# Diagonals of B written by DMA and loaded back, and a ring of states longer by a triple

## The chip, the cores and the metric

The kernel runs on one core of a Trainium2 chip. The metric is the device time of one execution in microseconds (us), lower is better; several runs are given by their median. The engines are PE (TensorE; PEld is its weight load), DVE (VectorE), ACT (ScalarE), POOL (GpSimd) and SP (SyncE), whose queue issues the DMAs.

## The reference

The input is x of 4 x 32 x 32 x 384, in f32. Two residual blocks follow each other.

```python
x = x + ssm_block(group_norm(x))        # conv + four-direction selective scan
x = x + moe_block(group_norm(x))        # router, top 2 of 4 experts, GELU
```

In the first block the projected input passes a 3 x 3 depthwise convolution and SiLU and becomes u. For each of 4 images and 4 directions (rows or columns, forward or backward) a selective scan over the 1024 positions is computed for 192 channels, with 16 states each:

```python
dA  = exp(dt[..., None] * A)                       # 192 channels x 16 states
h   = h * dA + (dt * u)[..., None] * B[:, None, :] # B: 16 values for a position
y   = einsum('bkcn,bkn->bkc', h, C)
```

B and C are projections of u and differ from position to position. Then follow a norm, a gate and a projection back. The second block's expert weights w1 and w2 are 384 x 384 each.

## The kernel before

There are three parts: `head` (norm, projection, convolution, projections of B, C and dt), `scan` and `tail` (norm and gate, output projection, experts).

`scan` handles 16 units, one for each image b, orientation o and direction s (unit u = 4b + 2o + s). A unit has 24 steps. Its 16 states are taken as 8 pairs n, and a pair with the 192 channels gives a triple of 3 steps (groups g of 64 channels, one state of the pair on each half of the partitions). All engines run their own instruction order and meet at semaphores:

- PE, `spread_b(u, i)`: (dt * u) times B, for the step's 128 partitions and 1024 positions, into the PSUM tile `pb` (two slots). B is applied by matmuls whose right side is a diagonal: for each state n and each of 8 blocks of positions (BLK = 8) the tile `dd` holds, on partition p of two halves of 64, row p of diag(B) (64 x 64 floats). `dd` is 128 partitions x 8192 floats and lies in `area`. A step is 32 such products (64 matmul records).
- DVE, `step_h(step)`: the scan itself, from `a` (the decay exp(dt A), made by ACT in `decay`) and `pb` into `h`. `h` has room for TRIPLES = 3 triples. Scan of triple n waits until triple n - TRIPLES has been added up (`y_added`).
- POOL, `times_c`: h times C, two instructions a triple; the rows of C come to `crow` by DMA (`load_crow`, 3 slots).
- PE, `add_y`: sums the triple into `py` and `py2` through an identity, LAG = 7 steps behind spread_b. It stands after spread_b of its step in PE's order.
- At the change of orientation `take_y` moves the sums out: at step 6, on DVE in units 2, 6, 10 and 14 (followed by `carry` on PE), on ACT in units 4, 8 and 12.

Beside a unit the next one is prepared, a chunk a step, PE into the PSUM tile `pm` and ACT out of it: Z (dt) at steps 0 to 3, BT (B with the positions on partitions, into `bt`) at step 4, UT (u; only before an even unit) at 5 to 8, DUP at 16 to 19. ACT does abs, exp and 1 + e at steps 4 to 6 and logarithms at 9, 11, 13; DVE does softplus at steps 9 to 14 and `times_u` (L294) after step 15.

The diagonals come from `bt` times `mask`, a constant with ones where j equals the partition (modulo 64). `dd` has four pieces of four states. POOL builds pieces 1 and 3 (`build_d`, L199, one instruction a piece), ACT pieces 0 and 2 (`build_rows`, L284, 32 instructions a piece, two or three a step). A piece is rebuilt when spread_b has used it up (6 steps a piece, `b_row`). For unit 0 pieces 0 and 1 are built in the head by POOL.

SP issues all DMAs in one written order. In the scan, for each n: crow, then at n = 0 the rows of dt and B of the next unit (`load_rows`) and sometimes u (`load_u`), at n = 3 sometimes `store_y`, at n = 7 `double`, a copy between halves of `dup`. crow of pair n waits until POOL is done with pair n - 3. Constants (KEPT) are loaded in the head, w1 and w2 among them.

Of the kernel before, what the change touches and what calls it, by code (L numbers as in the profile page):

```python
# [11 lines left out]
P = 128  # L12
BATCH = 4
# [18 lines left out]
PR = 32  # L32
KEPT = ("wout", "gam", "bet", "wr", "rb", "w1", "b1", "w2", "b2", "spread", "eyeb", "wdt", "apar", "dpar", "mask", "ones")
PROJ = 4
# [6 lines left out]
CROWS = 3  # L41
TRIPLES = 3
LAG = 7
# [4 lines left out]
Y_STORED = 16 * 3  # L48
LAST_U = UNITS - 1
KINDS = (2, 0, 1)  # L50
XD = ((0, 2, 1, 3), (0, 1, 2, 3))
# [63 lines left out]
def load_rows(sp, d, keep, shared, u):  # L115

    b, o, s = unit_of(u)
    rows = keep["rows"]
    sp.dma_start(rows[0:R], d["xd"][b, o, s * PR:s * PR + R]).then_inc(shared["rows_in"], 16)
    sp.dma_start(rows[PR:PR + N], d["xd"][b, o, 2 * PR + s * N:2 * PR + (s + 1) * N]).then_inc(shared["rows_in"], 16)  # L120

# [25 lines left out]
class Units:  # L147

    def __init__(self, nc, ctx, keep, ys, shared):
# [15 lines left out]
        self.dtut = sb("dtut", [P, 2, BLK, DI])  # L165
        self.bt = sb("bt", [P, 2, N, BLK])
        self.amin = sb("amin", [P, UNITS // BATCH * STEPS])
# [21 lines left out]
        self.d_odd = sem("d_odd")  # L189
        self.b_row = sem("b_row")  # L190
        self.dup_in = [sem(f"dup_in{g}") for g in range(CG)]

    def build_d(self, eng, tt, u, piece):

        eng.wait_ge(self.chunk_taken, CHUNK[u, "BT", 0] + 1)
        need(eng, self.b_row, STEPS * (u - 1) + 6 * (piece + 1) if u else 0)
        rows_n = slice(4 * piece, 4 * piece + 4)
        shape = [P, 4 * BLK, HALF]
        tt(self.dd[:, rows_n].rearrange("p n k j -> p (n k) j"),  # L199
           self.bt[:, u % 2, rows_n].rearrange("p n k -> p (n k)").unsqueeze(2).broadcast_to(shape),  # L200
           self.keep["mask"][:].unsqueeze(1).broadcast_to(shape), ALU.mult).then_inc(self.d_odd if piece % 2 else self.d_even, 1)
# [9 lines left out]
    def chunk(self, pe, u, what, i):  # L211
# [4 lines left out]
        if what == "Z":  # L216
            pe.wait_ge(self.shared["rows_in"], 16 * 2 * (u + 1))
# [23 lines left out]
    def take_chunk(self, act, u, what, i):  # L241

        nc, pm = self.nc, self.pm
        act.wait_ge(self.chunk_done, CHUNK[u, what, i] + 1)
        if what == "Z":
            need(act, self.dtu_ready, u)
            need(act, self.dt_ready, ROUNDS * u)
            dst, src = self.zs[:, 2 * DI * i:2 * DI * (i + 1)], pm[:, 0:2 * DI]
        if what == "BT":
            need(act, self.d_even, 2 * (u - 1))  # L250
            need(act, self.d_odd, 2 * (u - 1))
            dst = self.bt[:, u % 2].rearrange("p n k -> p k n")
# [23 lines left out]

    def build_rows(self, act, u, piece, lo, hi):

        if lo == 0:
            act.wait_ge(self.chunk_taken, CHUNK[u, "BT", 0] + 1)  # L280
            need(act, self.b_row, STEPS * (u - 1) + 6 * (piece + 1) if u else 0)
        for at in range(lo, min(hi, 4 * BLK)):
            n, blk = 4 * piece + at // BLK, at % BLK
            row = self.nc.scalar.activation(self.dd[:, n, blk], self.keep["mask"][:], ACT.Identity,  # L284
                                            scale=self.bt[:, u % 2, n, blk:blk + 1])
        if hi >= 4 * BLK:
            row.then_inc(self.d_even, 1)
# [111 lines left out]
def head(nc, d, keep, keep_from, ys, m, shared):  # L399
# [5 lines left out]
    with ExitStack() as ctx:  # L405
# [271 lines left out]
        def _(act):  # L677
# [111 lines left out]
            act.wait_ge(turned, NC * BATCH)  # L789
            m.build_rows(act, 0, 2, 0, 2 * BLK)  # L790

# [91 lines left out]
        def _(pool):  # L883
# [3 lines left out]
            for piece in range(2):  # L887
                m.build_d(pool, nc.gpsimd.tensor_tensor, 0, piece)


def scan(nc, d, keep, ys, m, norm, shared):

    with ExitStack() as ctx:
# [42 lines left out]
        def _(sp):  # L936
# [18 lines left out]
            for u in range(UNITS):  # L955
                b, o, s = unit_of(u)
                for n in range(NP):
                    load_crow(u * NP + n)
                    if n == 0 and u + 1 < UNITS:
                        sp.wait_ge(chunk_done, CHUNK[u, "BT", 0] + 1)  # L960
                        load_rows(sp, d, keep, shared, u + 1)
# [25 lines left out]
        def _(pe):  # L987
            def spread_b(u, i):
# [5 lines left out]
                if i % 6 == 0:  # L994
                    piece = i // 6
                    pe.wait_ge(d_odd if piece % 2 else d_even, 2 * u + piece // 2 + 1)
                need(pe, h_ready, step - 1)
# [67 lines left out]
        def _(act):  # L1065
# [29 lines left out]
            for u in range(UNITS):  # L1095
                b, o, s = unit_of(u)
                for i in range(STEPS):
# [3 lines left out]
                    if u + 1 < UNITS:  # L1101
# [85 lines left out]
        def _(pool):  # L1187
# [8 lines left out]
            for u in range(UNITS):  # L1196
                for n in range(NP):
                    times_c(u * NP + n, range(0, 2))
                    times_c(u * NP + n, range(2, CG))
                    if n == 1:  # L1200
                        m.build_d(pool, nc.gpsimd.tensor_tensor, u, 3)
                    if n == 4 and u + 1 < UNITS:
                        m.build_d(pool, nc.gpsimd.tensor_tensor, u + 1, 1)


def tail(nc, d, keep, ys, norm, shared):
# [8 lines left out]
    with ExitStack() as ctx:  # L1215
# [3 lines left out]
        def sem(name):  # L1219
            return ctx.enter_context(nc.semaphore("t_" + name))  # L1220

        eye, gavg, wout, gam, bet, wr, rb, w1, b1, w2, b2, spread, eyeb = (
            keep[k] for k in ("eye", "gavg", "wout", "gam", "bet", "wr", "rb", "w1", "b1", "w2", "b2", "spread", "eyeb"))
        yg = sb("yg", [P, KIND, L])
# [30 lines left out]

        xt_in = [sem(f"xt_in{b}") for b in range(BATCH)]
        small_taken = sem("small_taken")
        back_done = sem("back_done")
# [89 lines left out]
        def _(sp):  # L1348
# [23 lines left out]
        def _(pe):  # L1372
# [71 lines left out]

            def first_layer(b, j):
                for q in halves():
                    for c in range(NC):
# [17 lines left out]
            def second_layer(b, t):  # L1465
                if t == 0:
                    pe.wait_ge(hw_ready, NC * (b + 1))
                    pe.wait_ge(b2_ready, 5)
# [242 lines left out]
def kept(nc, ctx, d):  # L1711

    def sb(name, shape, dt=F32):
# [5 lines left out]
        gam=sb("gam", [P, DI]), bet=sb("bet", [P, DI]), wr=sb("wr", [P, NC, EXPERTS]), rb=sb("rb", [P, EXPERTS]),  # L1719
        w1=sb("w1", [P, NC, C]), b1=sb("b1", [P, NC]), w2=sb("w2", [P, NC, C]), b2=sb("b2", [PIECES * PR, C]),  # L1720
        spread=sb("spread", [PR, C], BF16),
# [10 lines left out]
    from_dram = dict(wout=d["wout"], gam=d["ln_g"].partition_broadcast(P), bet=d["ln_b"].partition_broadcast(P), wr=d["wr"],  # L1732
                     rb=d["rb"].partition_broadcast(P), w1=d["w1"], b1=d["b1"], w2=d["w2"], b2=d["b2"], spread=d["spread"],
                     eyeb=d["eyeb"], wdt=d["wdt"], apar=d["apar"], dpar=d["dpar"], mask=d["mask"], ones=d["ones"])
# [3 lines left out]
def bass_vision_mamba_moe(nc, x, eye, win, wx, gavg, conv_p, ones, wdt, apar, dpar, mask, wout, ln_g, ln_b, wr, rb, w1, b1, w2, b2, spread, eyeb, out):  # L1738
    def scratch(name, shape, dt=F32):
# [7 lines left out]
        xt=scratch("xt", (BATCH, NC, P, L)), sz=scratch("sz", (PAIRS, P, TT, 2 * DI)),  # L1747
        xd=scratch("xd", (BATCH, 2, P, L)), u=scratch("u", (PAIRS, KIND, P, L)), ub=scratch("ub", (PAIRS, 2, KIND, P, L)), y=scratch("y", (PAIRS, KIND, P, L)),
    )
# [110 lines left out]
```

## Time and profile before

| | |
|---|---|
| median of 3 runs | 1642.54 us (1640.47 to 1648.41) |
| profiled execution, its own time | 1650.07 us |
| its span, first to last instruction | 1648.3 us |
| busy: PE, PEld | 1349.6 us (82%), 824.1 (50%) |
| busy: DVE, ACT, POOL | 1229.3 (75%), 1014.8 (62%), 1026.4 (62%) |
| mean granted PE clock | 0.942 of full speed |
| DMA | 73478 packets, 151.08 MB, mean 92 GB/s |

Busy shares are means over stages with different limits. PE's records are pipelined, so its busy share is no measure of how full it is.

### The profile page before, as it was taken

What the parts mean: (1) busy time and instruction counts of PE and PEld (TensorE: products, weight loads), DVE (VectorE), ACT (ScalarE), POOL (GpSimd) and SP (SyncE); (2) the same over time, 40 slices, a digit from 0 to 9 for tenths busy, and PEclk for the clock granted to TensorE, in tenths of its full rate; (3) what the DMA queues carried; (4) which work ended last, traced back from release to release, by engine and by line L of the source; (5) the groups of instructions that cost most, each with busy time, mean ns of one, the idle gap of its engine ahead of it and who ended that gap; (6) DMA issues with size and microseconds to landing.
All of it is one profiled execution on the core that took longest, in us unless ns stands there. A gap on an engine that the chain in (4) does not pass through costs nothing. (4 is left out here: it accounts for less than half of the span.)

```text
span 1648.3 us, 66375 instructions
## 1 busy us (share of the span) xinstructions
PE 1349.6 (82%) x30408; PEld 824.1 (50%) x30408; DVE 1229.3 (75%) x1025; ACT 1014.8 (62%) x1916; POOL 1026.4 (62%) x294
## 2 busy tenths in 40 slices
PE   6997779687886979788697878869787867879998
PEld 5734546444554545455454545545454534436554
DVE  4984298979798897989889798888979884733220
ACT  2558578766777877677787767777776640402222
POOL 0002189879797988889798889979888870000000
PEclk8998689999999999999999999999999997879999
DMA  9334324323232432323343232324323325101101
GB/s 324 125 148 185 112 65 107 96 67 96 54 90 73 110 91 72 96 68 90 74 109 86 77 91 73 90 73 109 86 77 81 97 81 196 39 0 39 39 29 48
DMA packets 73478, 151.08 MB, mean 92 GB/s; under 512 B 33238, under 2 KB 41942, under 8 KB 72816
## 3 DMA queue, kind: packets, MB, share of 16 engines
q1 hardware_dynamic: 73200, 146.83, 30.3%
q8 instruction: 240, 3.93, 1.0%
q14 instruction: 38, 0.31, 0.1%
HBM read 101.72 MB, written 32.51 MB: 81 GB/s over the span
## 5 line engine op out<-in xcount | busy, mean ns | idle before, releaser
L1193 POOL TENSOR_TENSOR s_h<-s_h,s_crow 128x2048 f32<-128x2048 f32 (+1 forms) x256 | 880.2, 3469 | 198.0 <-DVE s_h L1158 197.9
L1158 DVE TENSOR_TENSOR_SCAN s_h<-s_a,s_pb 128x1024 f32<-128x1024 f32 x384 | 864.2, 2277 | 183.6 <-PE s_py L1041 78.5
L1002 PE MATMUL s_pb<-k_area,m_dtut 64*64 64x64 f32 x24576 | 470.2, 224 | 194.2 <-DVE s_h L1158 162.8
L1002 PEld LDWEIGHTS s_pb<-k_area,m_dtut 64*64 64x64 f32 x24576 | 424.1, 138 | 384.6 <-DVE s_h L1158 230.1
L1041 PE MATMUL s_py<-s_h,k_eye 64*64 64x512 f32 x3072 | 417.8, 603 | 20.4 <-ACT y_y L1090 15.6
L284 ACT ACTIVATE k_area<-k_mask,m_bt 128x64 f32<-128x64 f32 x992 | 273.9, 337 | 0.0
L1084 ACT ACTIVATE s_a<-y_y,m_aneg 128x1024 f32<-128x1024 f32 x192 | 218.6, 1139 | 39.9 <-DVE s_h L1158 39.8
L1084 ACT ACTIVATE s_a<-m_dup,m_aneg 128x1024 f32<-128x1024 f32 x192 | 219.5, 1143 | 29.7 <-DVE s_h L1158 29.7
L199 POOL TENSOR_TENSOR k_area<-m_bt,k_mask 128x2048 f32<-128x2048 f32 x33 | 145.8, 4419 | 126.1 <-ACT m_bt L262 126.1
L1041 PEld LDWEIGHTS s_py<-s_h,k_eye 64*64 64x64 f32 x3072 | 90.1, 137 | 33.3 <-ACT y_y L1090 16.0
L262 ACT COPY y_y<-m_pm 128x384 f32<-128x384 f32 (+1 forms) x96 | 49.2, 513 | 91.8 <-PE m_pm L219 79.2
L1070 ACT ACTIVATE m_pm<-y_y 128x512 f32<-128x512 f32 x45 | 26.8, 596 | 98.5 <-DVE y_y L1141 98.5
L219 PEld LDWEIGHTS m_pm<-k_wdt,k_rows 25*128 25x128 f32 x256 | 42.4, 196 | 56.9 <-issue 56.5
L1473 PE MATMUL t_small<-k_w,k_area 128*128 128x384 f32 x192 | 70.4, 504 | 0.0
L1538 ACT COPY t_out<-t_small 128x384 f32<-128x384 f32 x32 | 15.3, 479 | 88.4 <-PE t_small L1476 88.4
L1448 PE MATMUL t_big<-t_xn,k_w 128*128 128x512 f32 x144 | 67.9, 623 | 0.0
L219 PE MATMUL m_pm<-k_wdt,k_rows 25*128 25x192 f32 x256 | 62.5, 366 | 6.5 <-DMA k_rows<-scratch_xd 6.5
L805 DVE SCALAR_TENSOR_TENSOR h_acc<-h_xpad,h_conv_p,h_acc 128x1024 f32<-128x1024 f32 x48 | 61.7, 1285 | 1.6
L238 PEld LDWEIGHTS m_pm<-k_eye,y_y 64*64 64x64 f32 (+1 forms) x512 | 33.6, 123 | 52.9 <-issue 49.9
L1659 DVE TENSOR_TENSOR k_area<-k_area,t_big 128x1024 f32<-128x1024 f32 x12 | 14.3, 1219 | 50.6 <-PE t_big L1462 50.4
L1473 PEld LDWEIGHTS t_small<-k_w,k_area 128*128 128x128 f32 x192 | 37.0, 197 | 18.5 <-issue 1.9
L238 PE MATMUL m_pm<-k_eye,y_y 64*64 64x64 f32 (+1 forms) x512 | 42.9, 224 | 2.7 <-ACT y_y L262 2.7
(189 smaller groups left out, 1233.5 us busy)
## 6 DMA issues: line engine op xcount, KB each, us to landing
s_crow<-scratch_xd SPq DMA_DIRECT2D x256, 256.0 KB, 4.0
k_area<-in_x_dram SPq DMA_DIRECT2D x4, 1536.0 KB, 8.0
scratch_xt<-y_y SPq DMA_DIRECT2D x4, 1536.0 KB, 10.2
y_y<-y_y SPq DMA_DIRECT2D x24, 256.0 KB, 3.6
m_dup<-m_dup SPq DMA_DIRECT2D x24, 256.0 KB, 3.2
out_dram<-t_out SPq DMA_DIRECT2D x32, 192.0 KB, 1.9
k_area<-scratch_xt SPq DMA_DIRECT2D x3, 1536.0 KB, 6.9
scratch_xd<-h_dbl SPq DMA_DIRECT2D x8, 512.0 KB, 2.6
```

Source lines behind the costliest of these rows:

```text
L199: tt(self.dd[:, rows_n].rearrange("p n k j -> p (n k) j"), self.bt[:, u % 2, rows_n].rearrange("p n k -> p (n k)").unsqueeze(2).broadcast_ ...
L219: mm = pe.matmul(pm[:, x * DI:(x + 1) * DI], tokens(rows[0:R + 1], 2 * i + x), self.keep["wdt"][:, o + 2 * s], start=True, stop=True)
L238: mm = pe.transpose(pm[0:chans.stop - chans.start, blk::BLK], self.dt_of[here, blk, chans], eye[here, here])
L284: row = self.nc.scalar.activation(self.dd[:, n, blk], self.keep["mask"][:], ACT.Identity, scale=self.bt[:, u % 2, n, blk:blk + 1])
L805: eng.scalar_tensor_tensor(out, view, w, out, ALU.mult, ALU.add).then_inc(convolved[kind], 1)
L1002: mm = pe.matmul(pb[par * HALF:(par + 1) * HALF, step % 2, r * BANK + blk:(r + 1) * BANK:BLK], dtut[here, u % 2, blk, g * HALF:(g + 1) * H ...
L1041: mm = pe.matmul(dst, eye[here, here], src, start=opens, stop=closes)
L1084: nc.scalar.activation(a[:, step % RING], dup[u % 2][:, g], ACT.Exp, scale=aneg[:, col:col + 1]).then_inc(a_ready, 1)
L1158: nc.vector.tensor_tensor_scan(h[:, step % (TRIPLES * CG), f], a[:, step % RING, f], pb[:, step % 2, f], 0.0, ALU.mult, ALU.add).then_inc( ...
L1193: nc.gpsimd.tensor_tensor(here, here, c.unsqueeze(1).broadcast_to([P, groups.stop - groups.start, L]), ALU.mult).then_inc(hc_ready, 1)
L1448: mm = pe.matmul(big_of("F1", b, j)[:, q], w1[:, c, j * P:(j + 1) * P], xn[:, b % 2, c, q], start=(c == 0), stop=(c == NC - 1))
L1473: pe.matmul(ps, hid[:, j, tok], w2[:, j], start=False, stop=False, skip_group_check=True)
```

## The change

- `dd` is built on the core for unit 0 only. Its four pieces are then stored to a new DRAM tensor `dd` (`store_d`), so that all off the diagonals is zero there. For each later unit `write_diagonal` copies the 4 x 8 x 64 x 2 values of B of a piece from `xd` in DRAM onto the diagonals in DRAM (two DMAs of 2048 elements of 4 bytes, each element 8196 bytes after the one before), and `load_d` loads the piece (1 MB) into `area` when the unit before has used it up. Piece 0, 1 and 2 are written at n = 2, 4, 6 and loaded at n = 3, 5, 7 of the unit before, piece 3 at n = 0 and 1 of its own unit.
- `build_d` and `build_rows` remain for unit 0; the BT chunk and B's rows are no longer made for units 1 to 15, and `bt` has one slot.
- TRIPLES is 4, not 3.
- w1 and w2 are loaded in the tail, behind the loads of xt; PE waits for them before the first and the second expert layer.

```diff
-TRIPLES = 3
+TRIPLES = 4
+QUARTER = 4 * BLK * HALF
...
-    order = [("Z", ch) for ch in range(4)] + [("BT", 0)]
+    order = [("Z", ch) for ch in range(4)]
+    if u == 0:
+        order += [("BT", 0)]
...
+    def write_diagonal(self, sp, d, u, piece):
+        b, o, s = unit_of(u)
+        sp.wait_ge(self.d_stored[piece] if u == 1 else self.d_in[piece], 16 * max(u - 1, 1))
+        there = d["dd"][piece]
+        first = 2 * PR + s * N + 4 * piece
+        rows = d["xd"][b, o, first:first + 4].rearrange("n (k r j) -> r (n k) j", r=2, k=BLK)
+        for r in range(2):
+            diagonal = bass.AP(tensor=there.tensor, offset=there.offset + r * HALF * QUARTER, ap=[[HALF, 4 * BLK], [QUARTER + 1, HALF]])
+            sp.dma_start(diagonal, rows[r], allow_slow_non_contiguous=True).then_inc(self.d_written[piece], 16)
+
+    def load_d(self, sp, d, u, piece):
+        sp.wait_ge(self.d_written[piece], 32 * u)
+        sp.wait_ge(self.b_row, STEPS * (u - 1) + 6 * (piece + 1))
+        sp.dma_start(self.quarter(piece), d["dd"][piece]).then_inc(self.d_in[piece], 16)
+
+    def store_d(self, sp, d, piece):
+        sp.wait_ge(self.d_odd if piece % 2 else self.d_even, piece // 2 + 1)
+        sp.dma_start(d["dd"][piece], self.quarter(piece)).then_inc(self.d_stored[piece], 16)
...
+                    if u == 0 and n < 4:
+                        m.store_d(sp, d, n)
+                    if n in (2, 4, 6) and u + 1 < UNITS:
+                        m.write_diagonal(sp, d, u + 1, (n - 2) // 2)
+                    if n in (3, 5, 7) and u + 1 < UNITS:
+                        m.load_d(sp, d, u + 1, (n - 3) // 2)
+                    if n == 0 and u:
+                        m.write_diagonal(sp, d, u, 3)
+                    if n == 1 and u:
+                        m.load_d(sp, d, u, 3)
...
-                        if 6 <= i < 18:
-                            m.build_rows(act, u + 1, 0, share(i - 6), share(i - 5))
-                        if i >= 18:
-                            m.build_rows(act, u + 1, 2, share(i - 18), share(i - 17))
-                    if i < 6:
-                        m.build_rows(act, u, 2, share(i + 6), share(i + 7))
+                    if u == 0 and i < 6:
+                        m.build_rows(act, 2, share(i + 6), share(i + 7))
...
-                    if n == 1:
-                        m.build_d(pool, nc.gpsimd.tensor_tensor, u, 3)
-                    if n == 4 and u + 1 < UNITS:
-                        m.build_d(pool, nc.gpsimd.tensor_tensor, u + 1, 1)
+                    if u == 0 and n == 1:
+                        m.build_d(pool, nc.gpsimd.tensor_tensor, 3)
...
+            sp.dma_start(w1[:], d["w1"]).then_inc(w1_in, 16)
+            sp.dma_start(w2[:], d["w2"]).then_inc(w2_in, 16)
```

## Rows read from the trace of the kernel before

**Rows 1.** Line L1158, the scans: ns min/median/max, first and last start; idle before, us and times.

```profile
L1158 DVE TENSOR_TENSOR_SCAN s_h<-s_a,s_pb x384: 2255/2280/2289, 187.6 to 1342.8; 128x1024 f32<-128x1024 f32 x192
...
  PE s_py L1041: 78.5, 72
  PE s_pb L1002: 63.2, 43
```

**Rows 2.** Groups by line and shape: busy us, mean ns | idle before.

```profile
L1193 POOL TENSOR_TENSOR s_h<-s_h,s_crow 128x2048 f32<-128x2048 f32 x128 | 583.0, 4554 | 188.8 <-DVE s_h L1158 188.6
...
L1193 POOL TENSOR_TENSOR s_h<-s_h,s_crow 128x1024 f32<-128x1024 f32 x128 | 305.0, 2383 | 9.3 <-DVE s_h L1158 9.2
L284 ACT ACTIVATE k_area<-k_mask,m_bt 128x64 f32<-128x64 f32 x992 | 273.9, 337 | 0.0
...
L199 POOL TENSOR_TENSOR k_area<-m_bt,k_mask 128x2048 f32<-128x2048 f32 x33 | 145.8, 4419 | 126.1 <-ACT m_bt L262 126.1
```

**Rows 3.** Waits by engine, 229 to 1318 us: us in total, times, longest.

```profile
PE s_pb L1002 <- issue: 25.0, 30, 3.6
...
SPq L943 <- POOL s_h L1193: 725.6, 117, 11.7
```

**Rows 4.** Timeline of an odd unit, steps 4 to 9: start, us, instruction.

```profile
711.91 0.81 PE L1002 MATMUL s_pb<-k_area,m_dtut 64*64 64x64 f32 x39
...
714.46 1.16 PE L1002 MATMUL s_pb<-k_area,m_dtut 64*64 64x64 f32 x64
...
726.67 1.16 PE L1002 MATMUL s_pb<-k_area,m_dtut 64*64 64x64 f32 x64
...
727.65 1.04 PE L1041 MATMUL s_py<-s_h,k_eye 64*64 64x512 f32 x8
...
728.86 2.29 DVE L1158 TENSOR_TENSOR_SCAN s_h<-s_a,s_pb 128x1024 f32<-128x1024 f32 x1 [1.73 <-PE s_py L1041]
```

**Rows 5.** Timeline of unit 4, steps 5 to 8, with ACT's take_y and SP's y2 stores.

```profile
495.44 1.50 ACT L269 ACTIVATE y_y<-y_y 128x1536 f32<-128x1536 f32 x1
...
497.00 1.11 PE L1002 MATMUL s_pb<-k_area,m_dtut 64*64 64x64 f32 x64
...
497.93 1.04 PE L1041 MATMUL s_py<-s_h,k_eye 64*64 64x512 f32 x8
...
498.79 1.11 PE L1002 MATMUL s_pb<-k_area,m_dtut 64*64 64x64 f32 x64
...
503.56 0.99 ACT L1089 COPY y_y<-s_py 128x1024 f32<-128x1024 f32 x1
...
505.44 4.33 SPq L952 DMA_DIRECT2D scratch_y<-y_y  x2
...
508.72 2.29 DVE L1158 TENSOR_TENSOR_SCAN s_h<-s_a,s_pb 128x1024 f32<-128x1024 f32 x1 [5.12 <-PE s_pb L1002]
```

**Rows 6.** DMA issues of the span: count, size, median us to landing.

```profile
k_area<-scratch_xt SPq DMA_DIRECT2D x3, 1536.0 KB, 6.9
...
k_u<-scratch_ub SPq DMA_DIRECT2D x16, 128.0 KB, 5.1
...
scratch_y<-y_y SPq DMA_DIRECT2D x8, 128.0 KB, 6.1
```

**Rows 7.** Windows: length; busy PE, PEld, DVE, ACT, POOL; clock, DMA share, GB/s.

```profile
695.00:701.00 6.00, 3.66 (x127) 2.37 (x126) 5.55 (x3) 4.28 (x9) 6.00 (x3) 1.00 0.82 215
588.00:594.00 6.00, 4.04 (x144) 2.31 (x144) 5.93 (x7) 3.91 (x8) 5.81 (x2) 1.00 0.76 216
```

**Rows 8.** Timeline of PE at 695 to 702 us: what stood inside groups of spread_b.

```profile
695.55 0.50 PE L1002 MATMUL s_pb<-k_area,m_dtut 64*64 64x64 f32 x18 [0.91 <-issue]
...
701.10 0.74 PE L1002 MATMUL s_pb<-k_area,m_dtut 64*64 64x64 f32 x34 [1.89 <-issue]
```

**Rows 9.** Page, part 3, DMA queues: packets, MB, share of 16 engines.

```profile
q1 hardware_dynamic: 73200, 146.83, 30.3%
q8 instruction: 240, 3.93, 1.0%
```

More of the change, by code:

```diff
@@ L32 @@
 PR = 32
-KEPT = ("wout", "gam", "bet", "wr", "rb", "w1", "b1", "w2", "b2", "spread", "eyeb", "wdt", "apar", "dpar", "mask", "ones")
+KEPT = ("wout", "gam", "bet", "wr", "rb", "b1", "b2", "spread", "eyeb", "wdt", "apar", "dpar", "mask", "ones")
 PROJ = 4
@@ L119, in load_rows @@
     sp.dma_start(rows[0:R], d["xd"][b, o, s * PR:s * PR + R]).then_inc(shared["rows_in"], 16)
-    sp.dma_start(rows[PR:PR + N], d["xd"][b, o, 2 * PR + s * N:2 * PR + (s + 1) * N]).then_inc(shared["rows_in"], 16)
+    if u == 0:
+        sp.dma_start(rows[PR:PR + N], d["xd"][b, o, 2 * PR + s * N:2 * PR + (s + 1) * N]).then_inc(shared["rows_in"], 16)
 def load_u(sp, d, keep, shared, b, what):
@@ L165, in __init__ @@
         self.dtut = sb("dtut", [P, 2, BLK, DI])
-        self.bt = sb("bt", [P, 2, N, BLK])
+        self.bt = sb("bt", [P, N, BLK])
         self.amin = sb("amin", [P, UNITS // BATCH * STEPS])
@@ L190, in __init__, with build_d @@
         self.b_row = sem("b_row")
+        self.d_in = [sem(f"d_in{piece}") for piece in range(4)]
+        self.d_stored = [sem(f"d_stored{piece}") for piece in range(4)]
+        self.d_written = [sem(f"d_written{piece}") for piece in range(4)]
         self.dup_in = [sem(f"dup_in{g}") for g in range(CG)]
-    def build_d(self, eng, tt, u, piece):
-        eng.wait_ge(self.chunk_taken, CHUNK[u, "BT", 0] + 1)
-        need(eng, self.b_row, STEPS * (u - 1) + 6 * (piece + 1) if u else 0)
+    def build_d(self, eng, tt, piece):
+        eng.wait_ge(self.chunk_taken, CHUNK[0, "BT", 0] + 1)
         rows_n = slice(4 * piece, 4 * piece + 4)
@@ L216, in chunk @@
         if what == "Z":
-            pe.wait_ge(self.shared["rows_in"], 16 * 2 * (u + 1))
+            pe.wait_ge(self.shared["rows_in"], 16 * (u + 2))
             for x in range(2):
@@ L249, in take_chunk @@
         if what == "BT":
-            need(act, self.d_even, 2 * (u - 1))
-            need(act, self.d_odd, 2 * (u - 1))
-            dst = self.bt[:, u % 2].rearrange("p n k -> p k n")
+            dst = self.bt[:].rearrange("p n k -> p k n")
             src = pm[:, 0:BLK * N].rearrange("p (k n) -> p k n", k=BLK)
@@ L275, in exponent, with quarter, build_rows @@
             nc.scalar.activation(self.wz, ez, ACT.Identity, bias=1.0).then_inc(self.w_ready, 1)
-    def build_rows(self, act, u, piece, lo, hi):
+    def write_diagonal(self, sp, d, u, piece):
[14 more added lines that the diff above has]
+        sp.dma_start(d["dd"][piece], self.quarter(piece)).then_inc(self.d_stored[piece], 16)
+    def quarter(self, piece):
+        return self.keep["area"][:].rearrange("p a l -> p (a l)")[:, piece * QUARTER:(piece + 1) * QUARTER]
+    def build_rows(self, act, piece, lo, hi):
         if lo == 0:
-            act.wait_ge(self.chunk_taken, CHUNK[u, "BT", 0] + 1)
-            need(act, self.b_row, STEPS * (u - 1) + 6 * (piece + 1) if u else 0)
+            act.wait_ge(self.chunk_taken, CHUNK[0, "BT", 0] + 1)
         for at in range(lo, min(hi, 4 * BLK)):
@@ L284, in build_rows @@
             row = self.nc.scalar.activation(self.dd[:, n, blk], self.keep["mask"][:], ACT.Identity,
-                                            scale=self.bt[:, u % 2, n, blk:blk + 1])
+                                            scale=self.bt[:, n, blk:blk + 1])
         if hi >= 4 * BLK:
@@ L789, in _ @@
             act.wait_ge(turned, NC * BATCH)
-            m.build_rows(act, 0, 2, 0, 2 * BLK)
+            m.build_rows(act, 2, 0, 2 * BLK)
         def convolve(eng, pair, kind, taps=range(9)):
@@ L887, in _ @@
             for piece in range(2):
-                m.build_d(pool, nc.gpsimd.tensor_tensor, 0, piece)
+                m.build_d(pool, nc.gpsimd.tensor_tensor, piece)
 def scan(nc, d, keep, ys, m, norm, shared):
@@ L959, in _ @@
                     if n == 0 and u + 1 < UNITS:
-                        sp.wait_ge(chunk_done, CHUNK[u, "BT", 0] + 1)
+                        sp.wait_ge(chunk_done, CHUNK[u, "Z", 3] + 1)
                         load_rows(sp, d, keep, shared, u + 1)
@@ L995, in spread_b @@
                     piece = i // 6
-                    pe.wait_ge(d_odd if piece % 2 else d_even, 2 * u + piece // 2 + 1)
+                    if u == 0:
+                        pe.wait_ge(d_odd if piece % 2 else d_even, piece // 2 + 1)
+                    else:
+                        pe.wait_ge(m.d_in[piece], 16 * u)
                 need(pe, h_ready, step - 1)
@@ L1220, in sem @@
             return ctx.enter_context(nc.semaphore("t_" + name))
-        eye, gavg, wout, gam, bet, wr, rb, w1, b1, w2, b2, spread, eyeb = (
-            keep[k] for k in ("eye", "gavg", "wout", "gam", "bet", "wr", "rb", "w1", "b1", "w2", "b2", "spread", "eyeb"))
+        eye, gavg, wout, gam, bet, wr, rb, b1, b2, spread, eyeb = (
+            keep[k] for k in ("eye", "gavg", "wout", "gam", "bet", "wr", "rb", "b1", "b2", "spread", "eyeb"))
+        w1, w2 = sb("w1", [P, NC, C]), sb("w2", [P, NC, C])
         yg = sb("yg", [P, KIND, L])
@@ L1256, in tail @@
         xt_in = [sem(f"xt_in{b}") for b in range(BATCH)]
+        w1_in, w2_in = sem("w1_in"), sem("w2_in")
         small_taken = sem("small_taken")
@@ L1445, in first_layer @@
             def first_layer(b, j):
+                pe.wait_ge(w1_in, 16)
                 for q in halves():
@@ L1466, in second_layer @@
                 if t == 0:
+                    pe.wait_ge(w2_in, 16)
                     pe.wait_ge(hw_ready, NC * (b + 1))
@@ L1719, in kept @@
         gam=sb("gam", [P, DI]), bet=sb("bet", [P, DI]), wr=sb("wr", [P, NC, EXPERTS]), rb=sb("rb", [P, EXPERTS]),
-        w1=sb("w1", [P, NC, C]), b1=sb("b1", [P, NC]), w2=sb("w2", [P, NC, C]), b2=sb("b2", [PIECES * PR, C]),
+        b1=sb("b1", [P, NC]), b2=sb("b2", [PIECES * PR, C]),
         spread=sb("spread", [PR, C], BF16),
@@ L1732, in kept @@
     from_dram = dict(wout=d["wout"], gam=d["ln_g"].partition_broadcast(P), bet=d["ln_b"].partition_broadcast(P), wr=d["wr"],
-                     rb=d["rb"].partition_broadcast(P), w1=d["w1"], b1=d["b1"], w2=d["w2"], b2=d["b2"], spread=d["spread"],
+                     rb=d["rb"].partition_broadcast(P), b1=d["b1"], b2=d["b2"], spread=d["spread"],
                      eyeb=d["eyeb"], wdt=d["wdt"], apar=d["apar"], dpar=d["dpar"], mask=d["mask"], ones=d["ones"])
```

4 lines of the change are left out of this document (2 added, 2 removed).

## The prediction

> **What bounds the kernel now.** I read the windows by stage first. The scan stage, 384 scans from 187.6 to 1342.8 us, is 1155 of the 1648 us, 72.2 us for each of 16 units [rows 1]; all parts of the change but the move of w1 and w2 lie in it. Then the idle time before the scans. A scan takes 2.28 us, 24 of them fill 55 us of a unit. Some 9 more are waits: 78.5 us in all on add_y (py) and 63.2 on spread_b (pb), both of them TensorE [rows 1]. What is left is softplus and the product with u. The idle times of the others say who is no bound: GpSimd's work per triple is 4.55 + 2.38 us, about three scans, and before it GpSimd waited 188.6 us for the scans [rows 2]; SP's queue waited 725.6 us for GpSimd [rows 3].
>
> Then the timeline of one odd unit. While TensorE has a chunk to do behind each step (steps 0 to 8), its steps take 2.55 us (BT, from 711.91 to 714.46) to 3.05 (UT, four steps from 714.46 to 726.67), over the 2.28 of a scan: it is the bound there [rows 4]. In steps 9 to 14 VectorE does two softplus instructions behind each scan and TensorE waits. In steps 16 to 23 the two are about even: a bare step of TensorE is 1.79 us [rows 5], one with a DUP chunk lies above the scan.
>
> **What the change does to each.**
>
> *BT chunk gone from the 15 preparations after the first.* The step with it takes 714.46 - 711.91 = 2.55 us [rows 4], a bare one 498.79 - 497.00 = 1.79 [rows 5]. It stands where TensorE is the bound, so 0.76 x 15 = 11.4 us.
>
> *Ring of four triples.* Scan 3n waits now for add_y of triple n-3, which stands behind spread_b of its own step on TensorE; with four triples it needs only spread_b. Inside a stretch where TensorE is the bound this wins nothing: the wait on py becomes one on pb. What is won is at its end. Scan 9 of the odd unit began at 728.86, after add_y (from 727.65, 1.04 long); spread_b of that step began at 726.67 and took 1.16 us, so pb was there at 727.83 and the scan could begin near 728.0 [rows 4]. That is 0.85 x 7 odd units = 6.0. The 72 waits on py have a mean of 1.09 us, more than four a unit. In the 8 even units scan 9, just after the stop described below, has a short one; I take half the mean, 0.5: 4.0. Two more stand at steps 21 and 24 (0 of the next unit), where part of the wait is a late spread_b all the same: a third of the mean each, 0.7 a unit for 15 units, 10.5. Ceiling of all this is the 78.5 us [rows 1], floor zero.
>
> *ACT's 960 rows gone.* 992 rows cost 273.9 us, 0.276 each [rows 2]; ACT is mostly not the bound, so 265 us of its work are worth little. The exception is take_y on ACT, in units 4, 8 and 12. The last add_y that it needs begins at 497.93 and ends at 498.97, but ACT, busy without a gap from abs at 495.44, copies py at 503.56 only; scan 8 stands idle 5.12 us for it [rows 5]. In between lie 8 rows (3, 3 and 2), 2.2 us, and the copy out of the BT chunk goes too. The copy of py would come some 2.5 us earlier, of which 0.76 is counted: 1.8 x 3 = 5.4. In the four units where VectorE takes y it begins when scan 6 ends, which the ring moves by some 0.7 more: 2.8.
>
> *GpSimd's 30 builds gone.* 33 took 145.8 us [rows 2]. TensorE adds a triple 7 steps later, so they were absorbed, and GpSimd waits for VectorE more from now on. Zero; if that cover were gone, up to 4.4 us a build. The last unit, with waits of its own on py, gives 1. Sum of the gains: 11.4 + 6.0 + 4.0 + 10.5 + 5.4 + 2.8 + 1.0 = 41 us.
>
> *w1 and w2 moved.* 1.15 MB less in the head, where no wait for these loads shows; in the tail they queue on SP behind four xt loads (1.5 MB lands in 6.9 us [rows 6]) and before the load of y. In PE's order the first expert layer stands behind the whole projection of images 0 and 1, which hides some 5 us of loading, and the load of y waits for the gate of pair 0 in any case. Zero either way, 2 us if y comes late.
>
> *The new DMAs, all on SP's queue.* Per unit four loads of 1 MB, and four diagonals of 2 x 2048 elements of 4 bytes, from DRAM to DRAM. SP is passed through in this order: crow, diagonal at n = 0, 2, 4, 6; crow, load at n = 1, 3, 5, 7, and a load waits for its diagonal. Behind a waiting SP stand the next crow (POOL has two triples, some 14 us, before it misses it), rows and double. A load of 1 MB should land in about 5 us (1.5 MB in 6.9). Elements of 4 bytes do not occur in the trace. Nearest in number: the two y2 stores, 2048 runs of 64 bytes each, which took SP 4.33 us to issue [rows 5] and landed in 6.1 [rows 6]. Other bound: the halves of u2, 512 runs of 256 bytes read from DRAM, land in 5.1 [rows 6]; if each run cost the same, 2048 would take 20 us. The number of runs decides, I think, and the reading side adds something: I take 8 us. Then SP stays on time and all pieces land a quarter of a unit or more before use. The Trainium skill (DMA: Bandwidth & Descriptors, Rules for kernel authors) says that a last dimension that isn't contiguous becomes one descriptor per element; by it the diagonal is as bad as its number of elements, which the 8 us assume.
>
> *What these bytes do to TensorE.* Inside groups of 64 matmuls of one spread_b TensorE stands still with nothing that it waits for: 25.0 us in 30 stops [rows 3], 1.7 a unit. An example is 1.89 us at 701.10 [rows 8], right after the loads of rows and u, 0.82 of the DMA engines busy [rows 7]. The instructions come by DMA too, 3.93 MB in 240 packets [rows 9], and I take these stops for late instructions. The same DMA share (0.76 at 588 to 594 [rows 7]), with TensorE waiting for VectorE, costs nothing. Of the eight new transfers of a unit four (diagonal and load of piece 3, then of piece 0) fall into steps 21 to 8, where TensorE is the bound or close to it; the others are near steps 8 to 17, mostly hidden. Floor: zero. Ceiling: the 0.91 and 1.89 us around the example, 2.8, for two such bursts and 2 for the rest, 4.8 a unit, 72 us in all. I take 0.45 for each of the four, 1.8 a unit, nearer to today's 1.7 a unit for all transfers together: 27 us. The Trainium skill (Runtime: NRT & Kernel Launch, Instruction fetch mechanics) says that the fetch of a 16 KiB block is mostly hidden; by it this term is about nothing and the sum is the 41 us; the 25.0 us of stops speak against it.
>
> Sum: -41 + 27 = -14 us against the profiled execution's own 1650.07, so 1636 for it; the median of the runs shown is 1642.54, and the same difference gives 1628. The DMA share of the data queue, 30.3% [rows 9], should come to 50 to 65% of the scan.
>
> **Rivals.**
>
> *The stops stay as they are.* The bursts are spread out, and the time is 41 us down: 1601. For it: the loads of u at 588, step 11, left no mark [rows 7]. Against: that is where TensorE has time.
>
> *Gain and stops cancel.* 2.3 to 3.2 us of new stops a unit: between 1634 and 1650, no change to be told.
>
> *The instruction stream becomes the bound (slower).* Place: steps 21 to 8, spread_b. From 3.3 us a unit on (about 0.8 for each of the four bursts) the time rises over 1650; at the ceiling, 4.8, it is 72 - 41 = +31: 1673. For it: the example lost 2.8 us in 6 us. Against: the 4096 runs stored at 505 [rows 5] left no such stop.
>
> *The diagonals take too long for SP (slower).* Two triples last 72.2 / 4 = 18 us, and in them SP must issue two crows and a load (about 2 us) and wait a diagonal through. From 16 us a diagonal on GpSimd runs out of crows. At 20 us a unit takes 4 x 22.4 = 90, +17 x 15 = 260 us: about 1900. The Trainium skill (VectorE: DVE Perf Modes, The three transpose paths) calls a DMA that transposes by strides 19 times slower than the hardware's own when the destination step is large; no run here shows that.
>
> **How the numbers follow.** Half a per cent, 8 us, is about what a measurement of this kernel can tell from no change. Forecast (-8 to -30 us): 0.34. Stops unchanged: 0.14. Cancel: 0.22. Instruction stream: 0.21. Slow diagonals: 0.09. So faster 0.48, same 0.22, slower 0.30. The range goes from the second case's 1601 to the third's ceiling, 1672, and leaves out the slow diagonals and a little at each end; the likeliest case alone is 1612 to 1634.
>
> **What would show it.** Right: waits of the scans on py near 20 us instead of 78; a bare step of 1.8 us where BT was; the copy of py in units 4, 8, 12 about 2.5 us earlier in its unit; stops ("issue") before spread_b between 40 and 60 us; diagonals landing in 6 to 10 us; no wait of GpSimd on crow. Wrong: stops at 25 or over 75 us; GpSimd waiting for DMA; spread_b waiting for a load of its diagonals; a tail that waits for w1.

## The result, and the profile after

The changed kernel takes 1750.32 us (median, 1744.11 to 1757.88) against 1641.94 of the kernel before, now the median of four runs: ratio 1.064, 95% interval 1.060 to 1.068. I had forecast 1628 and a range of 1601 to 1672. All of the loss lies in the scan stage: from the first to the last scan before it was 1155 us [rows 1], now it is 1257. What follows the last scan did not grow (296 us of the span, 303 before).

The line of the scans after, with the idle time before them, answers to [rows 1]:

```profile
L1196 DVE TENSOR_TENSOR_SCAN s_h<-s_a,s_pb x384: 2255/2280/2290, 188.0 to 1445.3; 128x1024 f32<-128x1024 f32 x192
its engine sat idle before it (us, times) until:
  PE s_pb L1044: 241.9, 156
```

The scan itself is as long as before. The waits on py (78.5 us) are gone altogether, which is what the longer ring is for, but those on spread_b's pb have grown from 63.2 to 241.9 us.

The groups of lines after, two of them (to be held against [rows 2, 3]; columns as there):

```profile
L1231 POOL TENSOR_TENSOR s_h<-s_h,s_crow 128x2048 f32<-128x2048 f32 x128 | 582.4, 4550 | 402.3 <-DVE s_h L1196 395.8 <-issue 6.5
...
L1044 PE MATMUL s_pb<-k_area,m_dtut 64*64 64x64 f32 x24576 | 507.2, 230 | 241.6 <-issue 130.5 <-DVE s_h L1196 104.9 <-PEq L434 4.8
```

GpSimd waits for VectorE and never for crow: SP's queue is no bound. TensorE stands inside or before its groups of spread_b for 130.5 us with nothing that it waits for ("issue"), where it was 25.0 in the steady part [rows 3] and 25.4 over the whole span. Matmuls of 224 ns have become 230 in the mean: the granted clock over the scan stage fell as well, from 0.97 to 0.92, in the windows of that stage:

```profile
187.00:1440.00 1253.00, 986.40 (x28623) 624.88 (x28620) 1006.31 (x619) 612.75 (x692) 875.04 (x255) 0.92 0.57 133
```

The DMA share in it is 0.57, inside the 50 to 65% that I forecast. The DMA issues of the new kinds and the crow beside them (count, KB, median us to landing), and the data queue in the page's part 3:

```profile
q1 hardware_dynamic: 329616, 213.95, 48.2%
...
s_crow<-scratch_xd SPq DMA_DIRECT2D x256, 256.0 KB, 4.6
k_area<-scratch_dd SPq DMA_DIRECT2D x60, 1024.0 KB, 6.7
```

The diagonals' own DMAs land in 7.8 us at the median:

```profile
scratch_dd<-scratch_xd SPq DMA_DIRECT2D x120, 8.0 KB, 7.8
```

### The profile page after: what moved, and what is told of

Read it like the earlier page. It is cut to its first block and busy times, and to the rows that moved or that the text cites. A ratio compares the mean times of both kernels' runs of the same rounds, so it can differ in the third digit from the quotient of the medians.

```text
span 1743.7 us, 65301 instructions
## 1 busy us (share of the span) xinstructions
PE 1399.1 (80%) x30288; PEld 862.6 (49%) x30288; DVE 1234.3 (71%) x1025; ACT 792.1 (45%) x941; POOL 895.2 (51%) x264
## 3 DMA queue, kind: packets, MB, share of 16 engines
q1 hardware_dynamic: 329616, 213.95, 48.2%
## 5 line engine op out<-in xcount | busy, mean ns | idle before, releaser
L1196 DVE TENSOR_TENSOR_SCAN s_h<-s_a,s_pb 128x1024 f32<-128x1024 f32 x384 | 866.4, 2278 | 277.2 <-PE s_pb L1044 241.9
L1044 PE MATMUL s_pb<-k_area,m_dtut 64*64 64x64 f32 x24576 | 507.2, 230 | 241.6 <-issue 130.5
L1044 PEld LDWEIGHTS s_pb<-k_area,m_dtut 64*64 64x64 f32 x24576 | 462.5, 143 | 434.9 <-issue 271.6
L1083 PE MATMUL s_py<-s_h,k_eye 64*64 64x512 f32 x3072 | 457.5, 637 | 19.7 <-issue 12.8
L1083 PEld LDWEIGHTS s_py<-s_h,k_eye 64*64 64x64 f32 x3072 | 101.7, 143 | 39.5 <-issue 27.9
L205 POOL TENSOR_TENSOR k_area<-m_bt,k_mask 128x2048 f32<-128x2048 f32 x3 | 12.9, 4317 | 128.3 <-ACT m_bt L266 128.3
L225 PE MATMUL m_pm<-k_wdt,k_rows 25*128 25x192 f32 x256 | 67.5, 388 | 6.8 <-DMA k_rows<-scratch_xd 5.8
L1515 PE MATMUL t_small<-t_w,k_area 128*128 128x384 f32 x192 | 69.7, 500 | 0.0
L1489 PE MATMUL t_big<-t_xn,t_w 128*128 128x512 f32 x144 | 67.9, 623 | 0.0
L1515 PEld LDWEIGHTS t_small<-t_w,k_area 128*128 128x128 f32 x192 | 36.8, 196 | 18.1 <-issue 1.1
L1489 PEld LDWEIGHTS t_big<-t_xn,t_w 128*128 128x128 f32 x144 | 27.6, 198 | 33.7 <-issue 33.7
```

The lines of the kernel that those rows point to most:

```text
L1044: mm = pe.matmul(pb[par * HALF:(par + 1) * HALF, step % 2, r * BANK + blk:(r + 1) * BANK:BLK], dtut[here, u % 2, blk, g * HALF:(g + 1) * H ...
L1083: mm = pe.matmul(dst, eye[here, here], src, start=opens, stop=closes)
L1196: nc.vector.tensor_tensor_scan(h[:, step % (TRIPLES * CG), f], a[:, step % RING, f], pb[:, step % 2, f], 0.0, ALU.mult, ALU.add).then_inc( ...
L1489: mm = pe.matmul(big_of("F1", b, j)[:, q], w1[:, c, j * P:(j + 1) * P], xn[:, b % 2, c, q], start=(c == 0), stop=(c == NC - 1))
L1515: pe.matmul(ps, hid[:, j, tok], w2[:, j], start=False, stop=False, skip_group_check=True)
```

## The experiments

Times are medians; ratios are to the kernel before on the same chip, with their 95% interval. "Stops" are the time and number of TensorE's idle stretches before spread_b under "issue", from the waits of each run's profile over the whole span; for the kernel before they are 25.4 us in 31, for the changed one 130.5 in 86.

**1. No DMAs for the diagonals.**

```diff
-                    if u == 0 and n < 4:
-                        m.store_d(sp, d, n)
...
-                        m.load_d(sp, d, u, 3)
...
-                    else:
-                        pe.wait_ge(m.d_in[piece], 16 * u)
```

> The changed kernel without any of its DMAs for the diagonals: units 1 to 15 use the diagonals of unit 0, so B is wrong for them; all else (no BT chunk, no builds on ACT and POOL, four triples, w1 and w2 in the tail) as changed. If my sum of the gains is right and all of the loss lies in the DMAs: 41 us below the kernel before, about 1601. If the gains themselves were mis-sized: anything between 1601 and 1642. If something else in the change costs (the ring, the order on the engines): above 1642.

Measured: 1600.85 us, ratio 0.973 (0.968 to 0.977), stops 22.9 us in 22:

```profile
PE s_pb L1032 <- DVE s_h L1184: 144.0, 124, 1.9
PE s_pb L1032 <- issue: 22.9, 22, 2.4
```

The gains are there, at the size of my sum (1601). The DMAs, with what waits for them, cost the 149 us between 1601 and 1750.

**2. Loads only.**

```diff
-        sp.wait_ge(self.d_written[piece], 32 * u)
+        sp.wait_ge(self.d_stored[piece], 16)
...
-                    if n in (2, 4, 6) and u + 1 < UNITS:
-                        m.write_diagonal(sp, d, u + 1, (n - 2) // 2)
...
-                    if n == 0 and u:
-                        m.write_diagonal(sp, d, u, 3)
```

> The changed kernel with the stores of unit 0 and the 60 loads of 1 MB, but no element is written (each unit uses the diagonals of unit 0). Theory A, the bytes make the instructions late: most of the loss stays, 1700 or more, with some 90 us of stops inside spread_b. Theory B, the many small elements do it: near the kernel without the DMAs, within 20 us of it, stops near 30 us.

Measured: 1696.44 us, ratio 1.030 (1.025 to 1.036), stops 96.9 us in 55. The loads by themselves cost 95 us. The profile shows how. Its timeline of TensorE (start, us, instruction, idle before), and then its DMA queues in the windows 774:776 and 776:777:

```profile
773.63 0.68 PE L1040 MATMUL s_pb<-k_area,m_dtut 64*64 64x64 f32 x28
779.61 1.23 PE L1040 MATMUL s_pb<-k_area,m_dtut 64*64 64x64 f32 x35 [5.30 <-issue]
```

```profile
q1 hardware_dynamic: 101, 0.36, 97.5%
...
q1 hardware_dynamic: 22, 0.07, 25.5%
q8 instruction: 1, 0.02, 8.5%
```

A group of 64 matmuls breaks off after 28 and goes on 5.30 us later. A 1 MB load was issued at 768.45 and two copies of `double` behind it. While the data queue keeps all 16 engines 97.5% busy no packet of instructions is seen; in the window 776:777, as the data run out (25.5%), one comes. By the trace's packet records it runs from 776.98 to 778.35 us, the one before it ended at 765.72, and TensorE goes on at 779.61.

One such case could be chance, so here are all. Instruction packets of queue 8 are 16 KB. Of the 72 stops of 0.5 us or more before spread_b in the changed kernel each lies inside a group of 64, and each ends 1.1 to 2.1 us after the end of such a packet, 68 of them 1.2 to 1.8 us after; of moments spread evenly over the stage only 11% lie 1.2 to 1.8 us after the end of one. In run 2 it is 45 of 47 stops, in the kernel before 19 of 19. So TensorE goes on when an instruction packet has come. What these records don't tell is why a packet comes late; the experiments below bear on it.

**3. Diagonals only**, the loads and TensorE's wait for them taken out, and the next diagonal waiting for the last one.

```diff
-        sp.wait_ge(self.d_stored[piece] if u == 1 else self.d_in[piece], 16 * max(u - 1, 1))
+        sp.wait_ge(self.d_stored[piece] if u == 1 else self.d_written[piece], 16 if u == 1 else 32 * (u - 1))
...
-                    if n in (3, 5, 7) and u + 1 < UNITS:
-                        m.load_d(sp, d, u + 1, (n - 3) // 2)
...
-                    else:
-                        pe.wait_ge(m.d_in[piece], 16 * u)
```

> The changed kernel with its 120 DMAs of 2048 elements, but no loads (TensorE uses the diagonals of unit 0). Theory A, bytes: near the kernel without the DMAs, stops near 30 us. Theory B, elements: most of the loss stays, 1700 or more, stops near 90 us.

Measured: 1662.22 us, ratio 1.007 (1.003 to 1.011), stops 73.5 us in 61. So both theories had a part: the elements cost 61 us over run 1 and the loads 95, which would add up to 157; both together measured 149. (Both runs keep the four stores of unit 0, so what these cost is in both.) Neither alone is the cause.

**4. The same DMAs onto contiguous rows.**

```diff
-            diagonal = bass.AP(tensor=there.tensor, offset=there.offset + r * HALF * QUARTER, ap=[[HALF, 4 * BLK], [QUARTER + 1, HALF]])
+            diagonal = bass.AP(tensor=there.tensor, offset=there.offset + r * HALF * QUARTER, ap=[[HALF, 4 * BLK], [1, HALF]])
```

> The changed kernel in which each of the 120 DMAs writes its 2048 elements into one contiguous row of 8 KB and not onto a diagonal, so the same DMAs, waits and bytes without the small pieces (B is not placed rightly). Theory B, elements: falls to the time of the kernel with loads only. Theory A: stays near 1750.

Measured: 1680.18 us, ratio 1.020 (1.014 to 1.026), stops 88.5 us in 59. 120 small DMAs more than run 2, and not slower than it: what the diagonals cost is their pieces, not the number of DMAs, their waits or SP's order. They land in 3.4 us here and not in 7.8. Whether it is the number of the pieces or their spread over DRAM (8196 bytes apart) this run doesn't tell, since it takes both away.

**5. No DMAs and three triples.**

```diff
-TRIPLES = 4
+TRIPLES = 3
```

> The changed kernel without any of its DMAs for the diagonals (B of unit 0 in all units) and with three triples again. My terms for the ring are 6.0 + 4.0 + 10.5 + 2.8 + 1.0 = 24 us: about 1625, 24 above the kernel with four triples and without DMAs (1600.9). Rival, the ring is worth what the waits on py were, 60 us or more: 1660. Rival, nothing: 1601.

Measured: 1628.26 us (1611.72 to 1637.52), ratio 0.986 (0.981 to 0.990), 1.3 points above run 1: 21 us by the ratios, 27 by the medians. My 24 lie between, with runs that differ by more than that among themselves. The waits on py are back, 74.0 us in 62.

**6. The ring alone**, on the kernel before, with w1 and w2 in the tail.

```diff
-TRIPLES = 3
+TRIPLES = 4
```

> The kernel before with four triples (and w1 and w2 loaded in the tail, which makes the room); diagonals built on ACT and POOL as before. By my terms 24 us below before, about 1618 to 1624. If the ring only pays when POOL and ACT are relieved of the builds: within 5 us of before.

Measured: 1632.08 us, ratio 0.991 (0.988 to 0.995), 14 us faster by the ratio, 17 by the medians, where 24 was expected. Waits on py are gone here too, those on pb 128.7 us; the stops went up to 38.4 us in 37, which may be the difference but isn't shown to be.

**7. w1 and w2 alone.**

```diff
+            sp.dma_start(w1[:], d["w1"]).then_inc(w1_in, 16)
+            sp.dma_start(w2[:], d["w2"]).then_inc(w2_in, 16)
```

> The kernel before with only w1 and w2 moved to the tail. By my term zero, within 3 us of before. Rival: the tail after the last scan was 7 us shorter in the changed kernel; if that comes from this move, 5 to 8 us faster.

Measured: 1647.89 us, ratio 1.001 (0.998 to 1.004). Nothing, as my term had it. Nor is it this move that shortens what follows the last scan: that is 301 us here, 303 before and 296 in the changed kernel.

**8. The ring, and rows moved out of the way of take_y.**

```diff
+                late = s == 0 and o == 0 and u
...
+                        if late:
+                            if 9 <= i < 18:
+                                m.build_rows(act, u + 1, 0, 32 * (i - 9) // 9, 32 * (i - 8) // 9)
...
+                    if late:
+                        if i < 4:
+                            m.build_rows(act, u, 2, share(i + 6), share(i + 7))
+                        if i in (7, 8):
+                            m.build_rows(act, u, 2, share(i + 3), share(i + 4))
```

> The ring alone, and in units 4, 8 and 12, where ACT takes y at step 6, the rows of steps 4 to 6 are built at 7 and 8 and later, so that the copy of py isn't behind them. By my term for take_y some 1.5 us for each of three units, 5 us below the ring alone (the BT copy stays). If the copy waits for TensorE and not for ACT: the same as the ring alone.

Measured: 1623.04 us, ratio 0.986 (0.982 to 0.990), the fastest complete kernel of the study, faster than both that were compared. Over the ring alone it is 0.5 points, 8 us, with intervals that overlap, so the times can't tell my 5 us from nothing. The traces can: scan 8 of unit 4, which waits for take_y, stood idle 5.75 us in run 6 and stands 3.75 here,

```profile
501.37 4.47 DVE L1167 TENSOR_TENSOR_SCAN s_h<-s_a,s_pb 128x1024 f32<-128x1024 f32 x2 [3.75 <-PE s_pb L1002]
```

and in units 8 and 12 it is 3.71 and 3.53 in place of 5.82 each. The rows did stand in the way.

**9. The loads of run 2 at other places**: all four of a unit between steps 8 and 14.

```diff
+                    if n == 4 and u:
+                        sp.wait_ge(b_row, STEPS * u + 9)
+                        m.load_d(sp, d, u, 2)
+                    if n == 5 and u + 1 < UNITS:
+                        m.load_d(sp, d, u + 1, 0)
+                    if n == 6 and u:
+                        m.load_d(sp, d, u, 3)
+                    if n == 6 and u + 1 < UNITS:
+                        m.load_d(sp, d, u + 1, 1)
```

> Loads only, as in the run before with loads and no elements (1696), but all four loads of a unit issued between steps 8 and 14, where VectorE does softplus and TensorE waits for it. Theory A, a stop of TensorE costs only where TensorE has no time in hand: within 15 us of the kernel without DMAs, 1601 to 1616, though the bytes are the same and the stops may be as long. Theory B, the bytes cost wherever they are: 1680 or more.

Measured: 1633.0 us, ratio 0.992 (0.989 to 0.995): of the 95 us of the loads 32 are left, with the same bytes. The waits of TensorE:

```profile
PE s_pb L1045 <- issue: 74.5, 58, 5.1
PE s_pb L1045 <- DVE s_h L1197: 71.1, 65, 1.6
PE s_pb L1045 <- DMA k_area<-scratch_dd: 17.8, 4, 7.3
```

There are still 74.5 us of stops, 52 more than in run 1, but most of them are taken from TensorE's wait for VectorE, which fell from 144.0 to 71.1 us. 17.8 us are new: four times a piece came late, the price of loading it so close to its use. Where a stop falls matters as much as how long it is.

**10. All eight transfers at other places.** A complete kernel: loads as in 9, and the diagonals behind them at n = 4, 5 and 6.

```diff
+                    if n == 5:
+                        if u + 1 < UNITS:
+                            m.load_d(sp, d, u + 1, 0)
+                        if u:
+                            m.write_diagonal(sp, d, u, 3)
+                        if u + 1 < UNITS:
+                            m.write_diagonal(sp, d, u + 1, 1)
```

> The changed kernel, complete, with loads and diagonals issued in order between steps 8 and 16 of each unit. By theory A most of the 149 us of the DMAs is gone: 1605 to 1640, depending on how much of the diagonals' work runs on past step 15; under 1623 it beats the ring alone. By theory B it stays near 1750.

Measured: 1847.6 us, ratio 1.119 (1.115 to 1.124): far outside what either theory expected. SP's timeline of one unit (start, us until done, instruction) and TensorE's waits:

```profile
653.75 10.92 SPq L290 DMA_DIRECT2D scratch_dd<-scratch_xd  x4
...
671.66 2.36 SPq L972 DMA_DIRECT2D s_crow<-scratch_xd  x2
674.12 1.00 SPq L296 DMA_DIRECT2D k_area<-scratch_dd  x2
```

```profile
PE s_pb L1055 <- DMA k_area<-scratch_dd: 133.5, 17, 13.4
PE s_pb L1055 <- issue: 132.5, 67, 5.4
```

Two diagonals in a row hold SP for 10.92 us, and the load of piece 3 leaves at 674.12 only, when TensorE is about to need it at step 18: 133.5 us of waits for diagonals. Steps 16 to 23 take 34.5 us a unit, where the changed kernel has 22.0, while steps 0 to 8 went down from 31.5 to 27.2 (table below). This is near to the rival of the slow diagonals, brought about by my own order, but not the same: it is TensorE that waits for a load, and GpSimd waited for crow once, 3.3 us. It says nothing against run 9, and shows that in this order the window of 25 us doesn't hold all eight transfers.

**11. Each load in four parts.**

```diff
+        for part in range(4):
+            cols = slice(part * QUARTER // 4, (part + 1) * QUARTER // 4)
+            sp.dma_start(self.quarter(piece)[:, cols], d["dd"][piece][:, cols]).then_inc(self.d_in[piece], 16)
```

> Loads only, at their old places, each as four DMAs of 256 KB with rows of 2 KB in place of one with rows of 8 KB. If what makes the instructions late is that their packets wait behind long packets of data: half of the 95 us or more is gone, 1650 or less. If it is the bytes in the way: the same as the loads in one piece, 1696, within 10 us.

Measured: 1674.31 us, ratio 1.017 (1.013 to 1.021), stops 85.0 us in 49. 22 of the 95 us are gone: more than nothing, less than half. So the length of the rows, or whatever else four smaller DMAs change, has about a quarter of it.

**12. The loads from DRAM to DRAM.**

```diff
-        sp.dma_start(self.quarter(piece), d["dd"][piece]).then_inc(self.d_in[piece], 16)
+        sp.dma_start(d["dd2"][piece], d["dd"][piece]).then_inc(self.d_in[piece], 16)
```

> Loads only at their old places (1696), but each 1 MB goes from one DRAM tensor to another and not into SBUF; TensorE still waits for its semaphore, and uses the diagonals of unit 0. If the instructions are late because the DMA engines are taken: stops and time stay, 1670 to 1720. If writing into SBUF disturbs TensorE: near the kernel without DMAs, 1601 to 1615.

Measured: 1687.95 us, ratio 1.026 (1.018 to 1.034), stops 90.1 us in 71. None of the 60 MB goes into SBUF and TensorE stops all the same. It is the DMA engines (or DRAM), not SBUF.

**13. Half of each load.**

```diff
+        half = slice(0, QUARTER // 2)
+        sp.dma_start(self.quarter(piece)[:, half], d["dd"][piece][:, half]).then_inc(self.d_in[piece], 16)
```

> Loads only at their old places, half as many bytes each (rows of 4 KB in place of 8 KB; half of each piece stays that of unit 0). If the loss goes with the bytes in front of the instructions: about half of the 95 us, 1640 to 1655. If it comes with any burst, whatever its size: 1685 or more. If only what exceeds some lead of the fetch costs: less than a third of the 95 us, under 1632.

Measured: 1634.68 us, ratio 0.992 (0.988 to 0.996), stops 60.3 us in 61. Against run 1 that is 34 us for half of the bytes, 95 for all: of these two sizes the larger costs nearly three times the smaller. That lies between the expected cases, above "less than a third" and below "about half".

Bytes alone don't rank the runs. The time that the data queue's packets take, as the page's share of 16 engines times the span, is 491 us in run 1, 197 more in run 2 (67 MB more, 95 us lost), 166 more in run 3 (5 MB more, 61 us), 115 more here (36 MB, 34 us) and 350 more in the changed kernel (68 MB, 149 us). The small elements occupy the DMA engines nearly as long as the large loads do, and the loss goes with that rather than with the bytes.

The runs by part of the unit. I worked this out from the starts of the 384 scans in each trace: mean us of units 1 to 14 in steps 0 to 8 (chunks), 9 to 15 (softplus) and 16 to 23.

```
                            0-8    9-15   16-23
before                     28.3    24.9    19.9
1  no DMAs                 26.9    24.9    18.6
2  loads only              28.6    24.9    22.5
3  diagonals only          30.9    24.9    18.1
4  contiguous rows         29.6    25.0    21.4
9  loads at other places   26.7    25.5    19.4
10 all at other places     27.2    25.2    34.5
13 half loads              27.4    25.0    19.5
after                      31.5    24.9    22.0
```

## Why the prediction was wrong

**The gains** were right: 41 us forecast, 41 to 47 measured by run 1 (1600.85 against the 1641.94 of the first comparison, and against 1648.25 in its own). The ring's share, 24, is 21 to 27 by run 5, and 14 to 17 where the builds stay (run 6). w1 and w2 are worth nothing (run 7). TensorE's step where BT stood takes 1.84 us at the median in run 1 and 2.55 before, as forecast. That the sum came out so close is in part luck: the term for take_y was too small, since scan 8 of units 4, 8 and 12 stood idle 5.1 to 5.3 us before and 1.3 to 1.8 in run 1, 3.7 less where I had put 1.8 (2.5 with BT's part). What the builds on ACT and POOL are worth by themselves no run measured. The waits on py, which I put near 20 us, are none.

**SP and the diagonals' landing** were right: 8 us taken, 7.8 at the median, no wait of GpSimd on crow, none of TensorE on a load. The Trainium skill (DMA: Bandwidth & Descriptors, Rules for kernel authors) says one descriptor per element where the last dimension isn't contiguous, and the packets agree: 329616 in the data queue, and in run 2, without the diagonals, 81936:

```profile
q1 hardware_dynamic: 81936, 212.96, 40.7%
```

The difference is 247680, against 120 x 2048 = 245760 elements. But I had used that rule for the diagonal's own time alone. What the 245760 small packets do to others costs 54 to 70 us, by the pair of runs that one takes (61 between runs 1 and 3, 54 between run 2 and the changed kernel, 70 between run 4 and it).

**The step that failed** is "What these bytes do to TensorE": 27 us, ceiling 72, measured 149. The mechanism was the one named (the rival "The instruction stream becomes the bound"), and its price was mis-sized: 1.8 us a unit taken, 4.8 as the ceiling, 9.9 measured (149 over 15 units). The stops, 130.5 us, are past the 75 that I had set as a sign of being wrong. There are three reasons.

1. The price per burst. I took 0.45 us each, so that four came to the 1.7 us a unit that all transfers together cost before, most of them of 256 KB. Nothing ties that total to one transfer of 1 MB: run 13 shows that 1 MB costs nearly three times what 0.5 MB does. The two stops of 2.80 us together in [rows 8], after some 1 MB of rows, u and crow [rows 7], were the rows to go by, and I used them as a ceiling.
2. The place. I put four of the eight transfers where TensorE is the bound and the others "near steps 8 to 17, mostly hidden". That holds for steps 9 to 15, which are 24.9 or 25.0 us in every run of the table but 9 and 10 (25.5 and 25.2), though TensorE stops 20.2 us in them in run 2. It does not hold for step 17. All 15 loads of n = 7 in run 2 leave while TensorE is in its step 17, with `double` behind them, and 40.3 of its 96.9 us of stops lie in steps 19 and 20 (the one at 779.61 is such a stop). In the changed kernel the diagonals of n = 4 leave mostly in TensorE's steps 7 and 8 as well, so that six of the eight reach into the bound part, and not four. With loads only, steps 16 to 23 take 3.9 us a unit more than without DMAs, the most of any part (22.5 - 18.6).
3. The diagonals. I charged them as I charged the loads, and held the stores of y2 [rows 5], which had left no stop, against a higher price. But these were issued at 505.44, just after TensorE had stood for take_y:

```profile
505.08 1.88 PE L1041 MATMUL s_py<-s_h,k_eye 64*64 64x512 f32 x8 [5.19 <-ACT y_y L1090]
```

So the row says little of a TensorE that has been running; that the wait is why there was no stop isn't shown. In run 3 the diagonals cost 4.0 us a unit in steps 0 to 8 (30.9 - 26.9). Those of n = 2 leave there in TensorE's step 1 or 2, those of n = 4 mostly in 7 and 8; those of n = 0 leave in 21 to 23, and steps 16 to 23 are no longer than without them (18.1 against 18.6).

The Trainium skill (Runtime: NRT & Kernel Launch, Instruction fetch mechanics) calls the fetch mostly hidden. That agrees with the kernel without the new DMAs, 22.9 us of stops, and not with the changed one, 130.5: where the DMA engines are loaded the measurement decides.

The stops grew by 108 us over run 1 (130.5 - 22.9), but a stop of one microsecond isn't one microsecond lost (run 9), and stops aren't all. TensorE's account of the two profiled executions, 1743.7 and 1604.0 us, nearly closes: 107.6 us more of stops, 68.0 more of busy time for the same 30288 matmuls (1399.1 against 1331.1), 39.1 less of waiting for VectorE (104.9 against 144.0), together 136.5 of the 139.7. The busy time goes with the clock: TensorE was granted half of full speed (1.2 GHz) for 194 us of the scan stage, in run 1 for 66, and a group of 64 matmuls without a stop inside takes 1.91 us there in the mean and 1.19 at 2.4 GHz. That the stops bring the clock down isn't shown, as no run changes one without the other.

What stays open: why an instruction packet waits as long as it does. Run 12 rules SBUF out, run 11 leaves the length of the rows a small part. No run separates busy DMA engines from a busy DRAM as what keeps them; run 3, with 5 MB more than run 1 and 61 us lost, speaks for the engines. The order between the queues in a DMA engine wasn't tried. Nor is it shown why the ring alone has 13 us more of stops than the kernel before.

## What to carry to other kernels

A long unrolled kernel that keeps TensorE busy with small matmuls reads its instructions through the same DMA engines as its data, so work moved from an idle engine to DMA isn't free even if every transfer lands in time: here 41 to 47 us were gained and 149 lost. Before adding DMA traffic, look for "issue" stops inside groups of one line and for the largest transfer before them, and charge new bursts by that one, not by the mean. Count small elements by the time they take of the DMA engines, not by their bytes. Put large transfers where TensorE waits for another engine anyway (95 us became 32 in run 9), and take the part of such a change that needs no DMA: the longer ring and rows moved away from take_y, 1623 us.

## What I had not expected of the hardware

- TensorE stood still for up to 6.0 us in the middle of a group of matmuls, and for 130.5 us in all, at a DMA share of 0.57 of the stage.
- 60 loads of 1 MB cost 95 us, 60 of 0.5 MB 34 us, with landing times of 7.3 and 5.4 us that show nothing of it.
- The 120 DMAs of 2048 elements of 4 bytes from DRAM to DRAM move 1 MB in all and cost 61 us, nearly two thirds of what the 60 MB of loads cost.
- Every stop of 0.5 us or more before spread_b in the changed kernel ended 1.1 to 2.1 us after the end of a 16 KB packet of instructions.
